# Attention step of a four-layer kernel: the fourth transposed tile put behind the next step's scores, and value products behind the first two

## What is computed

```python
# layer 0 (a domain adapter)
hidden = gelu(x @ down_W.T + down_b)
hidden = hidden @ expert_W[id].T + expert_b[id] + domain_emb[id]
x = layernorm(hidden @ up_W.T + up_b + x) * ln_gamma + ln_beta
# layer 1 (attention, 16 heads of 32)
x = layernorm(x) * (1 + scale) + shift
q, k, v = x @ Wq + bq, x @ Wk + bk, x @ Wv + bv
scores = (q / sqrt(32)) @ k.T + attention_bias, masked keys at -inf
x = x + (softmax(scores) @ v) @ Wo + bo
# then a feed-forward block, layer 2 (an expert feed-forward with layernorm)
# and layer 3 (a stencil); neither is touched
```

## Time and profile before

| | us |
|---|---|
| median of 3 runs | 2863.32 |
| lowest, highest | 2859.99, 2865.2 |
| the profiled execution, its own time | 2858.26 |
| its span, first to last instruction | 2856.0 |
| TensorE busy in it | 2508.1 (88%) |
| VectorE, ScalarE, GpSimd busy | 2039.3, 1160.5, 1217.7 |
| mean granted TensorE clock | 0.956 of full |

### The profile page before, as it was taken

The page is one execution under the profiler, slowest core; times in us unless marked ns, Lnnn a source line. Parts: engine busy times, 40 slices in busy tenths (PEclk is TensorE's granted clock), DMA queues, the critical chain, the costliest instruction groups (busy, mean ns, idle before and its releaser), DMA issues.

```text
span 2856.0 us, 46535 instructions
## 1 busy us (share of the span) xinstructions
PE 2508.1 (88%) x14115; PEld 1211.6 (42%) x14203; DVE 2039.3 (71%) x3845; ACT 1160.5 (41%) x2197; POOL 1217.7 (43%) x1024
## 2 busy tenths in 40 slices
PE   2788888888888888884999999999999999999991
PEld 1344444444444444442444444444444444444440
DVE  4675756665757666676886878868788687886878
ACT  2465656565555656463232322323223232232321
POOL 3554454535353535452533425334253342433426
PEclk6799999999999999996999999999999999999995
DMA  3444444444444434435322223222232222322222
GB/s 132 136 134 131 148 132 133 132 120 138 126 140 124 138 127 133 132 104 179 129 89 88 89 81 118 89 83 94 81 111 92 85 94 83 111 89 88 92 67 80
DMA packets 155668, 319.38 MB, mean 112 GB/s; under 512 B 17714, under 2 KB 23474, under 8 KB 155458
## 3 DMA queue, kind: packets, MB, share of 16 engines
q1 hardware_dynamic: 145666, 299.13, 32.3%
q10 hardware_dynamic: 9792, 17.83, 1.7%
HBM read 298.85 MB, written 17.86 MB: 111 GB/s over the span
## 4 chain that ended last, share of the span: by engine, by line
PE 39%; issue 7%; DVE 4%; POOL 4%; ACT 1%; DMA 0%; SPq 0%; DVEq 0%; POOLq 0%; ACTq 0%
PE ffn_bank L1328 12%; PE ffn_bank L1330 12%; PE ffn_bank L1329 12%; PE ffn_bank L1321 2%; POOL prod L1249 1%; POOL f L1239 1%; POOL x L1267 1%; PE ffn_bank L1387 1%; PE ffn_bank L1337 0%; ACT g L1449 0%; DVE g2T_hi L1621 0%; DVE tmp L1530 0%; DVE tmp L1570 0%; DMA b<-in_b 0%; DVE g2T_lo L1622 0%
## 5 line engine op out<-in xcount | busy, mean ns | idle before, releaser
L935 DVE CUSTOM_DVE_ANT_0 tiles<-bank,bias 128x512 f32<-128x512 f32 x512 | 323.0, 687 | 221.3 <-PE bank L591 183.4
L751 ACT ACTIVATE tiles<-tiles,nmax 128x512 f32<-128x512 f32 x512 | 363.6, 712 | 249.2 <-DVE nmax L935 249.1
L490 POOL TENSOR_TENSOR bias<-bias,mask_add 128x1024 f32<-128x1024 f32 x128 | 272.0, 2136 | 342.4 <-DMA bias<-in_bias 333.1
L614 PE MATMUL bank<-ident,tiles 128*128 128x128 f32 x2048 | 286.7, 284 | 130.1 <-DVE pT L952 56.8
L614 PEld LDWEIGHTS bank<-ident,tiles 128*128 128x128 f32 x2048 | 223.4, 142 | 206.8 <-ACT tiles L751 80.2
L1621 DVE CAST g2T_hi<-g 128x512 f16<-128x512 f32 x256 | 189.0, 738 | 156.6 <-ACT g L1449 151.7
L1622 DVE TENSOR_TENSOR g2T_lo<-g,g2T_hi 128x512 f16<-128x512 f32 x256 | 270.0, 1055 | 8.8
L1449 ACT ACTIVATE g<-ffn_bank,bi 128x512 f32<-128x512 f32 x128 | 88.0, 687 | 360.4 <-PE ffn_bank L1330 323.0
L1249 POOL TENSOR_TENSOR prod<-grid,f 128x512 f32<-128x512 f32 x108 | 166.6, 1569 | 129.3 <-DMA grid<-in_grids 123.2
L1260 POOL TENSOR_TENSOR prod<-grid,f 128x512 f32<-128x512 f32 x64 | 105.4, 1667 | 265.6 <-DVE tmp L1559 144.7
L1328 PE MATMUL ffn_bank<-w_hi,g2T_hi 128*128 128x512 f16 x512 | 196.1, 383 | 23.8 <-DVE g2T_lo L1622 23.8
(11 more groups left out here) (256 smaller groups left out, 5125.2 us busy)
## 6 DMA issues: line engine op xcount, KB each, us to landing
bias<-in_bias SPq DMA_DIRECT2D x256, 512.0 KB, 4.2
raw<-in_W_l SPq DMA_DIRECT2D x128, 512.0 KB, 3.3
grid<-in_grids SPq DMA_DIRECT2D x172, 256.0 KB, 3.4
xin<-in_x SPq DMA_DIRECT2D x36, 256.0 KB, 4.2
x2n<-x_rows SPq DMA_DIRECT2D x9, 1024.0 KB, 7.1
out<-outt ACTq DMA_DIRECT2D x36, 256.0 KB, 2.0
x_rows<-tiles ACTq DMA_DIRECT2D x32, 256.0 KB, 3.0
l_rows<-in_rows SPq DMA_DIRECT2D x8, 768.0 KB, 4.4
```

The lines of the kernel that those rows point to most:

```text
L490: pool.tensor_tensor(bias[:, n % NB, :, :], bias[:, n % NB, :, :], mask_add[:, u % T, :].unsqueeze(1).to_broadcast([P, 2, S]), ALU.add).th ...
L614: mm = pe.transpose(bank[:, t * P:(t + 1) * P], tiles[:, 4 * (u % NR) + i, t * P:(t + 1) * P], ident[:, :])
L751: act.activation(tile, tile, ACT.Exp, scale=-1.0, bias=nmax[:, u % 2, i:i + 1], accum_out=rsum[:, j, h:h + 1]).then_inc(prob_ready, 1)
L935: dve.tensor_tensor_reduce(tiles[:, 4 * (u % NR) + i, :], bank[:, :], bias[:, half % NB, i % 2, :], -1.0, 3.0e38, ALU.add, ALU.min, nmax[: ...
```

## The change

Four things are changed, all in `attention_pass`.

1. `turn(u-1, 3)` leaves step u. It comes in step u+1 directly behind the scores, and ScalarE's copy of it comes first in its step u+1, ahead of the exps.
2. PE's value products stand between `turn(u-1, 1)` and `turn(u-1, 2)`. R is transposed in its turn in `BESIDE`.
3. The value projections v 2 and v 3 stand one step earlier, in steps 0 and 1.
4. `ACT_AFTER` replaces `TAKEN_AFTER`: in step 2 the products are now taken behind all four exps, in steps 0, 6 and 10 behind three, and R ahead of the exps. `DVE_AFTER` lets VectorE take the "up" products of steps 4 and 5 after two strips.

```diff
-BESIDE = {0: [("xT", 0), ("xT", 1)], 1: [("v", 2), ("xT", 2), ("xT", 3)],
-          2: [("v", 3), ("down",), ("q", 1)], 3: [("expert",), ("k", 1)], 4: [("up", 0), ("up", 1)],
-          5: [("up", 2), ("up", 3), ("R", 0)], 6: [("q", 2)], 7: [("k", 2)], 9: [("R", 1)], 10: [("q", 3)],
+BESIDE = {0: [("v", 2), ("xT", 0), ("xT", 1)], 1: [("v", 3), ("xT", 2), ("xT", 3)],
+          2: [("down",), ("q", 1)], 3: [("expert",), ("k", 1)], 4: [("up", 0), ("up", 1)],
+          5: [("R", 0), ("up", 2), ("up", 3)], 6: [("q", 2)], 7: [("k", 2)], 9: [("R", 1)], 10: [("q", 3)],
           11: [("k", 3)], 13: [("R", 2)], 17: [("R", 3)]}
 
-TAKEN_AFTER = {1: 3, 2: 3, 3: 2, 6: 2, 10: 2}
+ACT_AFTER = {0: 3, 1: 3, 3: 2, 5: 0, 6: 3, 9: 0, 10: 3, 13: 0, 17: 0}
+DVE_AFTER = {4: 2, 5: 2}
...
-        keys = BESIDE.get(u, []) + ([("T", u - 1, i) for i in range(4)] if 0 < u <= NQ else [])
+        keys = [("T", u - 2, 3)] if 1 < u <= NQ + 1 else []
+        keys += BESIDE.get(u, []) + ([("T", u - 1, i) for i in range(3)] if 0 < u <= NQ else [])
...
                     if u < NQ:
                         scores(u)
+                    if 1 < u <= NQ + 1:
+                        turn(u - 2, 3)
                     for key in BESIDE.get(u, []):
                         if key[0] in ("q", "k", "v"):
                             project(key)
-                        elif key[0] != "R":
+                        elif key[0] == "R":
+                            spread(key[1])
+                        else:
                             l0_products(it, key)
+                    if 0 < u <= NQ:
+                        turn(u - 1, 0)
+                        turn(u - 1, 1)
                     if u == NQ + 1:
                         out_products(0)
                         out_products(1)
                     for v, kb in pv_parts(u):
                         values(v, kb)
-                    for g in range(G):
-                        if ("R", g) in BESIDE.get(u, []):
-                            spread(g)
                     if 0 < u <= NQ:
-                        for i in range(4):
-                            turn(u - 1, i)
+                        turn(u - 1, 2)
...
                 for u in range(SLOTS_ALL):
+                    if 1 < u <= NQ + 1:
+                        evacuate(u - 2, 3)
                     for i in range(5):
-                        if i == TAKEN_AFTER.get(u, 4):
+                        if i == ACT_AFTER.get(u, 4):
                             for key in BESIDE.get(u, []):
                                 take(key)
...
                     if 0 < u <= NQ:
-                        for i in (2, 3):
-                            evacuate(u - 1, i)
+                        evacuate(u - 1, 2)
...
-                    for i in range(4):
+                    for i in range(5):
                         n = 4 * u + i
-                        if u < NQ:
+                        if i == DVE_AFTER.get(u, 4):
+                            for key in BESIDE.get(u, []):
+                                take(key)
+                        if i < 4 and u < NQ:
...
-                    for key in BESIDE.get(u, []):
-                        take(key)
```

## The result

| | us |
|---|---|
| after, median of 4 runs | 2779.73 (2775.53 to 2787.3) |
| before, on the same chip | 2861.65 (2859.36 to 2865.2) |
| ratio | 0.9713, 95% interval 0.969 to 0.9736 |
| the profiled execution after: its time, its span | 2787.3, 2785.5 |

The profiled execution is the highest of the four. On profiled executions the change is 2858.3 to 2787.3, -71; on the medians -82.

The account below looks back on a forecast made before the run. PE was taken to end the step, standing before full banks where engines could overlap. Terms summed to 8.75 us a sequence, 70 over eight: 2788 on the profiled execution, 2793 on the median; range 2757 to 2832.

Parts of the forecast that it names:

- Steps 8 and 9, the waits go: PE's tile waits for VectorE's copy in step 8 and for R in step 9 vanish: +1.75 and +2.10 us a sequence.
- The ring: Banks 4 to 6, three for four tiles a step: step 8's fourth tile waits 1.75 us for the first's bank.
- Steps 12 and 13, VectorE binds, 11.5 us from scores 12 to 14: VectorE, busy without a gap for 7.04 us, limits these steps: 11.5 us where it was 14.36, +2.9 a sequence.
- Steps 4 and 5: VectorE takes the "up" results after two strips, so PE's waits for them go: +1.7 us a sequence.
- Steps 15 to 19: Value products of step 15 wait for a copy behind ScalarE's four scalings, 2.0 us lost; -2.4 a sequence in all.
- Step 14 and the clock: A wait in step 14 goes, +0.8 us; fewer low-clock stretches in 9 and 13, longer waits in 2 and 15, +0.6.
- steps 6, 7, 10 and 11: A projection stands beside these steps and PE's own work fills them: 0 gained.
- rival B: The clock stays up once the waits of steps 8, 9, 12, 14 go: another 2.5 us a sequence, 2770; chance 0.14.
- Steps 0 to 3: A chain from expert weights through gelu to tile (1,3) sets the end; PE waits about 3.7 us; +1.3 a sequence.
- A: VectorE binds every light step: about 4 us a sequence gained, 2831; chance 0.20.
- C: Tile (u-2,3)'s copy holds value products in every odd step: 5 us a sequence slower, about 2905; chance 0.05.
- D: Bias loads bind and steps stay as they are: no change, 2863; chance 0.03.

Follow-up runs that it names:

- the two runs on tile 3: Tile 3's move alone on the kernel before, 2828.4 us; the kernel after with tile 3 and its copy put back, 2826.74 us.
- The run that puts the takes back: Kernel after, with VectorE taking the "up" products of steps 4 and 5 after all four strips again: 2800.61 us, ratio 0.9792.
- The split run: Kernel after, with ScalarE's four scalings of step 14 divided, two there and two at the end of step 15: 2774.65 us, ratio 0.9681.
- gelu one exp sooner: Kernel after, with ScalarE taking the products of step 2 after three exps and not four: 2767.8 us, ratio 0.9657.
- only tile 3: Kernel before, with only tile 3 moved behind the next scores and its copy first in ScalarE's step: 2828.4 us, ratio 0.9868.
- all but tile 3: Kernel after, with tile 3 back behind tile 2 of its own step, with its copy: 2826.74 us, ratio 0.9884.
- v back: Kernel after, with value projections v 2 and v 3 back in steps 1 and 2, gelu again behind three exps: 2755.03 us, ratio 0.9636.
- the wait on GpSimd: Kernel after, with GpSimd's bias add of step 6 waiting until VectorE has split the expert output: 2772.49 us, ratio 0.9699.

## Why the prediction was right

2793 was forecast, 2779.7 measured; by its own sum 70 us on the profiled execution, and 71 were measured. The mechanism of steps 8 to 15 was right. That the sum came out so closely is in part luck, as the points show:

- *Steps 8 and 9, the waits go*: right, +1.8 and +2.45 for 1.75 and 2.10. The ring and R's late copy as their causes are shown by the two runs on tile 3.
- *Steps 12 and 13, VectorE binds, 11.5 us from scores 12 to 14*: 11.36, with VectorE's last strip as the releaser. Right.
- *Steps 4 and 5*: +1.5 for 1.7, and partly luck. The short sequences gain 2.3; the long ones lose 1.4 of it in step 4, 0.9 on the mean. The run that puts the takes back shows 2.2 in short sequences.
- *Steps 15 to 19*: the wait ahead of the value products 1.96 for 2.0, the tile's 0.77 for 0.75; -2.3 for -2.4. The split run moves this wait and so confirms the scalings as its cause.
- *Step 14 and the clock*: mis-sized. Step 14 gave +1.5 where +0.8 was forecast: scores 14 took 2.09 at the low clock, and that loss ended. So did the one behind step 9's wait, in step 10 (7.63 to 7.14), most of the +0.7 of steps 6, 7, 10 and 11. Together that is 2.3, where step 14 and the clock were put at 1.4. Here rival B was right in its mechanism, and from step 5 to step 15 the clock no longer falls; but it added 0.9 a sequence and not the 2.5 that B put on it, and the clock now falls in step 4 of the long sequences.
- *Steps 0 to 3*: the term that failed, 0.0 for +1.3. No term of the prediction held GpSimd and VectorE against each other. The +1.3 is met in the three short sequences (38.4 to 37.1), where VectorE's split came ahead of GpSimd's add. In the five long ones it is -0.7, and 1.4 more are lost in step 4. "I find each link of it at the same distance after the change" was wrong as well. The fourth expert instruction met GpSimd's add and took 2.12 us in place of 0.29, all five 6.53 in place of 5.81: the adds end 19.03 us behind the first scores and not 18.27, since v 2 in step 0 puts the transposes they wait for later. The gelu follows a fourth exp instead of the shorter v copy. Together it comes 0.7 later. PE gets there 3 us sooner and waits 5.07, not 3.7. So even in the short sequences the +1.3 isn't the sum of its links as forecast.
- The sum came out on the profiled execution because the misses cancel: 1.3 too much in steps 0 to 3 against 0.9 too little for step 14 and the clock together and 0.35 too little in step 9, the rest being small.
- *On the median* the change was 82 and not 70. The prediction took the median 5 us above the profiled execution, as before; after, it lies 7.6 below.
- *Rivals.* A, VectorE binding everywhere: no, only steps 12 and 13. C, the stall in every odd step: only in 15. D, loads: the bias waits didn't bind. The Trainium skill (TensorE: Matmul & The Clock Gate, "A second HAM failure mode: psum-queue depth-cycling") names frequent small idles as what makes the clock swing; steps 5 to 15, where most such waits are gone and the granted clock is 1.00, agree.
- *Small slips*: 124.1 us over 7.6 sequences is 16.3 and not 16.4, and the three releasers that are named make 13.4 of it; B's 2.5 a sequence would be 2773 and not 2770.

What the prediction did not see at all is that a part of the change loses time. It costed the places of the value projections and of the gelu with all else as a net gain. Their price, 25 us together, about half of it the gelu's, is only visible when they are moved back.

What stays open is the longer tail with the gelu one exp sooner, and what in full brings the split and the add together. Their order alone decides the kind. In the kernels whose split leads by 0.9 us or more (the kernel before, only tile 3, all but tile 3, v back, gelu one exp sooner, the wait on GpSimd) no sequence is long. So the starts come within some 0.4 us of each other only with tile 3 moved and the gelu behind four exps; whether the place of the value projections is needed too isn't shown, since v back moves the gelu as well. Then their scatter decides. The add starts when its load has landed; why that moment scatters was not measured.

## What to carry to other kernels

A saved wait is worth its length only where nothing else ends the step: undo each part of a bundled change by itself, and again after the bound has moved, since the value projections and the gelu put back gained 3.6 us a sequence with one neighbour and lost 2.5 with another. Price an instruction on a chain by what its neighbour engine does at that moment, not by its size: five small VectorE instructions cost 1.6 or 6.5 us. And where runs of one kernel differ from sequence to sequence, look for two engines that race for something; a wait on the one that isn't due made every sequence here a short one, and the runs steady.

## What the runs showed of the hardware

- VectorE and GpSimd exclude each other on some instructions, and the first to start wins. The split with two SBUF inputs (line 848) took 0.69 us alone and 2.66 behind GpSimd's add, ending 0.55 us after it; the other way round the add took 2.38 and not 2.13. The five expert-weight instructions took 0.22 to 0.35 each alone, up to 2.24 beside adds. The Trainium skill (SBUF — State Buffer, "Who interferes with whom") says that a VectorE instruction with two SBUF inputs contends with a GpSimd instruction that reads SBUF, and that issue order decides who blocks; the trace agrees with both. It agrees for the one-input forms 836 and 847 as well (0.23 to 2.04, 0.43 to 1.68), which the page counts in when they run in a two-port mode; no trace shows the mode.
- The granted clock fell in step 1 behind waits of 1.34 and 0.49 us in some sequences and not in others, at the same waits, and did not fall behind 1.76 in step 13 with PE busy on both sides. Around the end of the 5.07 wait (step 2) it was low in both sequences that were looked at, 0.68 (555 to 560 us) and 0.64 (269 to 273.8).
